# Feed-forward input transposes grouped by row tile instead of by column pair, in a decoder layer on one core

## The chip, the core and the metric

The kernel runs on one NeuronCore of a Trainium2 chip. The metric is the device time of one execution in microseconds (us). TensorE (PE in the profile; PEld is its weight load) multiplies matrices into PSUM, VectorE (DVE) and ScalarE (ACT) read PSUM and SBUF, GpSimd (POOL) works on SBUF, and SyncE (SP) issues nearly all DMA transfers. Each engine works through its own instructions in order and waits on semaphores for the others.

## What is computed

A decoder layer: each of three blocks is added to its input after a layer norm. The first is causal self-attention with ternary weights, the second attention over a context, the third a feed-forward block that sends each row to the best of eight low-rank experts.

```
x = x + self_attention(layernorm(x))                    # x: 16 x 256 x 1024, f32
x = x + cross_attention(layernorm(x), ctx, ctx)         # 16 heads of 64, causal
z = layernorm(x)
logits = z @ Wr.T + br                                  # Wr: 8 x 1024
weight, expert = max, argmax of softmax(logits)
h = einsum('nd,erd->ner', z, A)                         # A: 8 x 64 x 1024
y = einsum('ner,eor->neo', h, B) / 64                   # B: 8 x 1024 x 64
x = x + y[n, expert[n]] * weight
```

## The kernel before

The kernel has two halves, one after the other. The first (`self_attention`) does the self-attention and fills the time up to about 1650 us. The second (`second_half`, from line 1128) does the cross-attention and the feed-forward block, and the change is in it alone.

**Numbers.** A float32 value is held as two float16 halves, high and low, and a product is three float16 matmuls (`split_product`, L71 is its matmul). A transposed tile is made in PSUM; then ScalarE writes the high half to SBUF (`high`, L1493) and VectorE subtracts it from the bank for the low half (`low`, L1639), which frees the bank.

**Tiling.** One batch element has 256 rows, so two row tiles of 128, and 1024 columns, so eight column blocks of 128. It takes a *round* of eight steps, s0 to s7. Step g = 8b + s works on head pair s of batch element b: `scores` (L87, L91) on TensorE, the masked maxima on VectorE (L101), the exponentials on ScalarE (L108), the high halves of the probabilities on ScalarE (L1532) and the low ones on GpSimd (L1582), their transpose by DMA (L1315), and three steps later the weighted sums on TensorE (L118). Each of these engines runs one loop over g, written out by hand.

**Feed-forward in the same loop.** The tables `EXTRA` (TensorE), `HIGH_AHEAD` (ScalarE) and `LAST` (VectorE) say what of the feed-forward block of an earlier batch element goes into which step. In s5 TensorE does scores, weighted sums, the expert product e2 and then the transposes of the normalised input x3 into four PSUM banks, `("x", b, k)` for k = 0 to 3. In s6 it does scores, weighted sums and e3; in s7 scores, `logits` and weighted sums, then the first half of the hidden product h0, whose rest is in s0. `t0`, `t1` are the transposes of the hidden rows, `e0` to `e3` the products with B. All of these results go through five PSUM banks in a fixed turn (`claim`, `bank`, `freed`).

**The normalised tiles.** For batch element f, VectorE takes the statistics in s3, GpSimd the reciprocal root (L1560, L1563) in s4, and ScalarE writes x3, row tile 0 at the end of s4 and row tile 1 at the start of s5 (`norm_apply`, L1514), with a copy of the next values (L1508) between the two. Each raises `ln_done` by one. Before each of its four groups of transposes TensorE waits for both tiles:

```
if kind == "x":
    pe.wait_ge(ln_done, 2 * b + 2)
    transposes(x3, ("x", b, k))
```

A bank k holds column blocks 2k and 2k + 1 of both row tiles. So x3T, the transposed input, is filled by pairs of column blocks: `x3T[:, 0, 2k:2k+2, :]`, 512 numbers in a row for each partition. ScalarE copies the four banks in s6 ahead of the exponentials of s6, VectorE subtracts them in s6 after the maxima and the normalised sums. `logits` (s7) waits until the last of the four banks is freed, then multiplies row tile 0 and row tile 1 of x3T with the router's weights (L71, into ps_o): 24 products each.

**Keys and probabilities.** The context of batch element b + 1 is split into halves by ScalarE and GpSimd in s3 and s4, and SP transposes it by DMA into kT, one row tile in s5 and one in s6 (`transpose_keys`, L1348), ahead of the probabilities' transpose of the same step. In s6 a load of the following context (L1360) stands between. SP issues the probabilities' transpose of step g after GpSimd's low halves and after the weighted sums of g - 2. `scores` in s0 waits for the keys.

Of the kernel before, what the change touches and what calls it, by code (L numbers as in the profile page):

```python
# [14 lines left out]
ACT = mybir.ActivationFunctionType  # L15
AX = mybir.AxisListType

P = 128
NB = 16
T = 256  # L20
NT = T // P
# [43 lines left out]
def split_product(pe, out, lhs, rhs, n_tiles, part=None, exact=None):  # L65


    for a in part or range(n_tiles):
        terms = [t for t in ((0, 1), (1, 0), (0, 0)) if a > 0 or exact is None or t[exact] == 0]
        for t in terms:  # L70
            last = pe.matmul(out, lhs(t[0], a), rhs(t[1], a), start=a == 0 and t is terms[0],  # L71
                             stop=a == n_tiles - 1 and t == (0, 0))
    return last
# [1054 lines left out]
def second_half(nc, consts, banks, scratch, queries, ctx, begun, left, yT_last, out):  # L1128
    ident, mask = consts
# [7 lines left out]
    def sb(name, shape, dt=F32):  # L1137
        return st.enter_context(nc.sbuf_tensor(name, shape, dt))

    def sem(name):  # L1140
        return st.enter_context(nc.semaphore(name))
# [63 lines left out]
    with st:  # L1205
# [36 lines left out]
        x3T = sb("x3T", [P, 2, DT, T], F16)  # L1242
# [18 lines left out]
        j_ready = sem("j_ready2")  # L1261
        j_free = [sem(f"j_free2_{k}") for k in range(NBANK)]
        hi_done = sem("hi_done2")
# [14 lines left out]
        ln_done = sem("ln_done2")  # L1278
# [8 lines left out]
        def bank(c):  # L1287
            return ps_j[place[c] % NBANK]

        def ready(c):  # L1290

            return len([o for o in order[:place[c] + 1] if o[0] != "o"])

        def freed(c):

            return j_free[place[c] % NBANK], place[c] // NBANK + 1
# [86 lines left out]
        @block.tensor  # L1383
        def _(pe):
            def claim(c):
                if place[c] >= NBANK:
                    pe.wait_ge(*freed(order[place[c] - NBANK]))
                return bank(c)

            def transposes(src, c):  # L1390
                to = claim(c)
                for a in range(2):
                    for n in range(NT):
                        last = pe.transpose(to[:, bass.ts(a * NT + n, P)],
                                            src[:, n, bass.ts(2 * c[2] + a, P)], ident[:])
                last.then_inc(j_ready, 1)

            def scores(g):
                b, t = g // NPAIR, g % NPAIR
                slot = b % 2  # L1400
                if t == 0 and b > 0:
                    pe.wait_ge(*keys_in(b))
                    if b < NB - 1:
                        pe.wait_ge(qT_in[slot], 16 * ((b + 1) // 2))
                    else:
                        pe.wait_ge(q_last_in, 16 * NT)
                if g > 0:
                    pe.wait_ge(max_done, 4 * g)
                causal_scores(pe, ps_s,
                              lambda i, r, n: qT[slot][r, n, bass.ts(DT * i + t, P)],  # L1410
                              lambda i, r: kT[r, slot, i, t], s_ready)

            def weighted_sums(g):
                b, t = g // NPAIR, g % NPAIR
                if t == 0 and b > 0:
                    pe.wait_ge(v_done, 2 * b)
                if g > 0:
                    pe.wait_ge(y_done, g)
                pe.wait_ge(*transposed(g))
                for e in range(2):  # L1420
                    last = weights_times_values(pe, ps_o[:, e],
                                                lambda i, k: probT[:, g % 2, e, i, k],
                                                v[:, b % 2].rearrange(
                                                    "p n i (h d) -> p i n h d", d=HD),
                                                2 * t + e, HD)
                last.then_inc(o_ready, 1)

            def logits(f):
                pe.wait_ge(*freed(("x", f, 3)))
                pe.wait_ge(y_done, min(NPAIR * (f + 2) - 1 - SUMS, GP))  # L1430
                for n in range(NT):
                    last = split_product(pe, ps_l[:, n],
                                         lambda i, a: x3T[:, i, a, bass.ts(n, P)],
                                         lambda i, a: rT[:, i, a, :], DT)
                last.then_inc(l_ready, 1)

            def hidden(f, n, part):
                to = claim(("h", f, n)) if part is FIRST else bank(("h", f, n))
                last = split_product(pe, to[:], lambda i, a: x3T[:, i, a, bass.ts(n, P)],
                                     lambda i, a: aT[:, i, a, :], DT, part)  # L1440
                if part is SECOND:
                    last.then_inc(j_ready, 1)

            def hidden_transposes(f, n):
                to = claim(("t", f, n))
                pe.wait_ge(*freed(("h", f, n)))
                for a in range(ERT):
                    last = pe.transpose(to[:, bass.ts(a, P)], hg[:, n, bass.ts(a, P)], ident[:])
                last.then_inc(j_ready, 1)

            def expert_out(f, j):
                n, half = j // 2, j % 2
                to = claim(("e", f, j))
                pe.wait_ge(*freed(("t", f, n)))
                split_product(pe, to[:], lambda i, a: hT[:, i, n, a, :],
                              lambda i, a: bT[:, i, a, bass.ts(half, BANK)], ERT) \
                    .then_inc(j_ready, 1)

            def out_projection(j, a):
                to = claim(("o", NB - 1, j)) if a == 0 else bank(("o", NB - 1, j))  # L1460
                if (j, a) == (0, 0):
                    pe.wait_ge(yT_last, 16 * NT)
                last = split_product(pe, to[:], lambda i, a: yT[:, i, a, bass.ts(j // 2, P)],
                                     lambda i, a: woT[:, half_tile(i, a), bass.ts(j % 2, BANK)],
                                     DT, (a,), exact=1)
                if a == DT - 1:
                    last.then_inc(out_ready, 1)

            for g in range(GEND):
                if g < GP:  # L1470
                    scores(g)
                if g % NPAIR == NPAIR - 1 and 0 <= g // NPAIR - 1 < NB:
                    logits(g // NPAIR - 1)
                if 0 <= g - SUMS < GP:
                    weighted_sums(g - SUMS)
                for j, a in out_parts.get(g, []):
                    out_projection(j, a)
                for kind, b, k, part in listed(EXTRA, g):
                    if kind == "x":
                        pe.wait_ge(ln_done, 2 * b + 2)  # L1480
                        transposes(x3, ("x", b, k))
                    elif kind == "h":
                        hidden(b, k, part)
                    elif kind == "t":
                        hidden_transposes(b, k)
                    else:
                        expert_out(b, k)

        @block.scalar
        def _(act):  # L1490
            def high(dst, c):
                act.wait_ge(j_ready, ready(c))
                act.activation(dst, bank(c)[:], ACT.Copy).then_inc(hi_done, 1)  # L1493

            def pair(k):
                return slice(2 * k, 2 * k + 2)

            def high_of(c):
                kind, b, k = c
                if kind == "t":  # L1500
                    return hT[:, 0, k]
                return x3T[:, 0, pair(k), :]

            def values(b, n):
                act.wait_ge(ctx_in, 16 * b)
# [4 lines left out]
            def norm_apply(f, a):  # L1510
                act.wait_ge(ln_pow, 2 * f + 2)
                if f > 0:
                    act.wait_ge(j_ready, ready(("x", f - 1, 3)))
                act.activation(x3[:, a, :], x2[f % 3][:, a, :], ACT.Identity,  # L1514
                               scale=rstd[:, a:a + 1], bias=offset[:, a:a + 1]) \
                    .then_inc(ln_done, 1)
# [100 lines left out]
        def _(dve):  # L1617
# [18 lines left out]
            def low(dst, hi, c):  # L1636
                dve.wait_ge(hi_done, halves_done(c))
                src = bank(c)[:].rearrange("p (a n) -> p a n", a=hi.shape[1])
                dve.tensor_tensor(dst, src, hi, ALU.subtract).then_inc(freed(c)[0], 1)  # L1639

            def low_pair(to, c):
                a = slice(2 * c[2], 2 * c[2] + 2)
                low(to[:, 1, a, :], to[:, 0, a, :], c)

            def add_expert_out(f, j):
                c = ("e", f, j)
# [167 lines left out]
```

## Time and profile before

| | |
|---|---|
| median of 3 runs | 2278.14 us (2277.64 to 2280.89) |
| profiled execution | 2285.66 us |
| its span, first to last instruction | 2283.4 us |
| mean granted TensorE clock in it | 0.968 |
| TensorE busy | 2063.9 us (90%) |
| VectorE busy | 1642.1 us (72%) |
| ScalarE busy | 1172.9 us (51%) |
| GpSimd busy | 975.8 us (43%) |
| DMA, mean over the span | 163 GB/s |

All durations are of the one profiled execution. Busy shares are means over two halves with different loads: the second half begins at about 1650 us. The granted clock is the share of TensorE's full speed that the chip allowed in a stretch: 1.00 is 2.4 GHz, 0.50 is 1.2 GHz. Matmuls are pipelined, so a run of n of them is read from the start of one group to the start of the next. In a chain of waits each piece was released by the piece above it.

### The profile page before, as it was taken

How to read it: one execution, taken by the hardware profiler on the slowest of the kernel's cores; microseconds unless marked ns; L12 is line 12 of the kernel's file. 1: busy time of each engine (PE TensorE's matmuls, PEld its weight loads, DVE VectorE, ACT ScalarE, POOL GpSimd, SP SyncE). 2: the span in 40 equal slices, each digit the busy share in tenths (PEclk: the TensorE clock that was granted, in tenths of full speed). 3: DMA queues.
4: the chain of work that ended last, by engine and by line, in shares of the span. 5: the costliest groups of instructions: out<-in, count | busy, mean ns of one | idle time of the engine just before them, and what ended most of it. 6: DMA issues, size and time to landing. Idle time of an engine off the chain costs nothing. (4 is left out here: it accounts for less than half of the span.)

```text
span 2283.4 us, 52017 instructions
## 1 busy us (share of the span) xinstructions
PE 2063.9 (90%) x19320; PEld 1329.2 (58%) x19320; DVE 1642.1 (72%) x4595; ACT 1172.9 (51%) x3114; POOL 975.8 (43%) x919
## 2 busy tenths in 40 slices
PE   1657899999999999999999999997789899988978
PEld 1435566666666666666666666665345555554544
DVE  7877678777777777787777777766566667676664
ACT  6976434333433333333334334334677767686761
POOL 4333334334433333343343333433565656565651
PEclk9878999999999999999999999998899999999999
DMA  9977665665657666556556566568999999999862
GB/s 240 196 157 150 133 145 132 145 143 134 151 123 160 140 139 137 144 131 157 140 135 152 124 160 134 123 160 213 223 203 221 204 230 211 223 215 216 186 131 73
DMA packets 800572, 372.82 MB, mean 163 GB/s; under 512 B 746553, under 2 KB 746809, under 8 KB 800321
## 3 DMA queue, kind: packets, MB, share of 16 engines
q1 hardware_dynamic: 800320, 369.50, 71.1%
q8 instruction: 154, 2.52, 0.5%
q14 instruction: 98, 0.79, 0.1%
HBM read 104.11 MB, written 49.28 MB: 67 GB/s over the span
## 5 line engine op out<-in xcount | busy, mean ns | idle before, releaser
L108 ACT ACTIVATE prob<-prob,negmax 128x128 f32<-128x128 f32 (+1 forms) x1024 | 428.5, 444 | 175.0 <-DVE negmax L101 173.7
L905 POOL TENSOR_TENSOR halves<-prob,halves 128x384 f16<-128x384 f32 x256 | 239.7, 937 | 583.8 <-ACT halves L829 583.8
L71 PE MATMUL ps_j<-xT,wT 128*128 128x256 f16 x3634 | 416.6, 275 | 24.6 <-DMA wT<-rows_qkv 24.6
L101 DVE CUSTOM_DVE_ANT_0 prob<-ps_s,mask 128x128 f32<-128x128 f32 (+1 forms) x1024 | 304.3, 353 | 170.2 <-PE ps_s L91 170.0
L71 PEld LDWEIGHTS ps_j<-xT,wT 128*128 128x128 f16 x3634 | 359.0, 99 | 85.3 <-issue 24.8
L1062 DVE TENSOR_TENSOR raw<-raw,cos 128x512 f32<-128x512 f32 x128 | 140.4, 1097 | 249.7 <-DMA swp<-raw 249.7
L818 ACT ACTIVATE raw<-ps_j,factor_qk 128x256 f32<-128x256 f32 x158 | 66.2, 470 | 451.0 <-PE ps_j L71 451.0
L1582 POOL TENSOR_TENSOR halves<-prob,halves 128x768 f16<-128x768 f32 x128 | 210.7, 1646 | 174.1 <-ACT halves L1532 174.1
L71 PE MATMUL ps_t<-xT,wT 128*128 128x256 f16 x2254 | 255.5, 273 | 0.0
L71 PEld LDWEIGHTS ps_t<-xT,wT 128*128 128x128 f16 x2254 | 221.3, 98 | 36.4
L71 PE MATMUL ps_j<-wT,yT 128*128 128x512 f16 x897 | 205.4, 385 | 0.0
L71 PE MATMUL ps_j<-wT,xT 128*128 128x512 f16 x874 | 196.4, 381 | 0.0
L818 ACT ACTIVATE raw<-ps_t,factor_qk 128x256 f32<-128x256 f32 x98 | 41.1, 471 | 288.4 <-PE ps_t L71 288.4
L1064 DVE TENSOR_TENSOR swp<-swp,sin 128x512 f32<-128x512 f32 x128 | 172.4, 1347 | 0.0
L876 POOL TENSOR_TENSOR small<-small 128x1 f32<-128x1 f32 x62 | 34.4, 554 | 312.8 <-DVE small L1007 312.8
L71 PE MATMUL ps_t<-wT,xT 128*128 128x512 f16 x598 | 139.6, 391 | 7.6 <-DMA wT<-rows_qkv 7.6
L71 PEld LDWEIGHTS ps_j<-wT,yT 128*128 128x128 f16 x897 | 85.4, 99 | 98.2 <-issue 4.9
L899 POOL TENSOR_TENSOR yh<-y,yh 128x256 f16<-128x256 f32 x128 | 130.7, 1021 | 22.6 <-ACT yh L808 22.6
L71 PEld LDWEIGHTS ps_j<-wT,xT 128*128 128x128 f16 x874 | 83.4, 98 | 95.4 <-issue 2.1
L829 ACT ACTIVATE halves<-prob 128x384 f16<-128x384 f32 x256 | 133.8, 523 | 8.1
L71 PE MATMUL ps_t<-wT,yT 128*128 128x512 f16 x575 | 129.5, 381 | 0.0
L1532 ACT ACTIVATE halves<-prob 128x768 f16<-128x768 f32 x128 | 108.0, 843 | 37.4 <-DMA probT<-halves 34.0
(194 smaller groups left out, 3594.1 us busy)
## 6 DMA issues: line engine op xcount, KB each, us to landing
swp<-raw SPq DMA_DIRECT2D x512, 64.0 KB, 2.0
xin<-in_x SPq DMA_DIRECT2D x33, 512.0 KB, 4.4
kv_ahead<-in_ctx SPq DMA_DIRECT2D x16, 1024.0 KB, 6.3
x_kept<-after_self_attention SPq DMA_DIRECT2D x16, 1024.0 KB, 5.8
xres<-in_x SPq DMA_DIRECT2D x31, 512.0 KB, 4.3
after_self_attention<-xres SPq DMA_DIRECT2D x30, 512.0 KB, 3.3
queries<-q2T SPq DMA_DIRECT2D x30, 512.0 KB, 3.1
out<-x SPq DMA_DIRECT2D x10, 1024.0 KB, 5.0
```

The lines of the kernel that those rows point to most:

```text
L71: last = pe.matmul(out, lhs(t[0], a), rhs(t[1], a), start=a == 0 and t is terms[0], stop=a == n_tiles - 1 and t == (0, 0))
L101: dve.tensor_tensor_reduce(scores[:, cols], bank[:, cols], hidden, scale, NO_SCORE, ALU.add, ALU.min, least[:, n:n + 1]).then_inc(done, 1)
L108: last = act.activation(prob[:, cols], prob[:, cols], ACT.Exp, scale=-1.0, bias=least[:, n:n + 1], accum_out=None if sums is None else sum ...
L818: last = act.activation(raw[:, g % 2, w], bank(("qk", g, 0))[:, bass.ts(w, T)], ACT.Copy, scale=factor_qk[:, w, t:t + 1])
L829: act.activation(halves[:, e, 0, :], prob[:, e], ACT.Copy) \
L876: pool.tensor_tensor(rstd[:], rstd[:], minus_half[:], ALU.pow).then_inc(ln_pow, 1)
L899: pool.tensor_tensor(yh[:, :, 1, pair], y[:, g % 2], yh[:, :, 0, pair], ALU.subtract).then_inc(y_lo, 1)
L905: pool.tensor_tensor(halves[:, e, 1, :], prob[:, e], halves[:, e, 0, :], ALU.subtract).then_inc(prob_lo, 1)
L1062: dve.tensor_tensor(z, z, cos[:].unsqueeze(1).broadcast_to([P, 2, T]), ALU.mult) \
L1064: dve.tensor_tensor(swp[:], swp[:], sin[:].unsqueeze(1).broadcast_to([P, 2, T]), ALU.mult).then_inc(sin_done, 1)
L1532: act.activation(halves[:, g % 2, :, 0, :], prob[:, g % 2], ACT.Copy) \
L1582: pool.tensor_tensor(halves[:, g % 2, :, 1, :], prob[:, g % 2], halves[:, g % 2, :, 0, :], ALU.subtract).then_inc(prob_lo, 1)
```

## The change

A bank of the transposes now holds four column blocks of one row tile: banks 0 and 1 row tile 0 (blocks 0 to 3 and 4 to 7), banks 2 and 3 row tile 1. TensorE waits for tile 0 alone before banks 0 and 1, and for both before banks 2 and 3. ScalarE and VectorE write each bank to four pieces of 128 numbers in x3T, 256 apart. `logits` waits for banks 0 and 1 before row tile 0 and for banks 2 and 3 before row tile 1. ScalarE's `norm_apply` waits only for the transposes that read its own tile. The number of transposes, banks, copies and subtractions and their order are unchanged.

```diff
             def transposes(src, c):
+
+                n, first = c[2] // 2, 4 * (c[2] % 2)
                 to = claim(c)
-                for a in range(2):
-                    for n in range(NT):
-                        last = pe.transpose(to[:, bass.ts(a * NT + n, P)],
-                                            src[:, n, bass.ts(2 * c[2] + a, P)], ident[:])
+                for a in range(4):
+                    last = pe.transpose(to[:, bass.ts(a, P)],
+                                        src[:, n, bass.ts(first + a, P)], ident[:])
                 last.then_inc(j_ready, 1)
...
             def logits(f):
-                pe.wait_ge(*freed(("x", f, 3)))
                 pe.wait_ge(y_done, min(NPAIR * (f + 2) - 1 - SUMS, GP))
                 for n in range(NT):
+                    for k in (2 * n, 2 * n + 1):
+                        pe.wait_ge(*freed(("x", f, k)))
                     last = split_product(pe, ps_l[:, n],
...
                     if kind == "x":
-                        pe.wait_ge(ln_done, 2 * b + 2)
+                        pe.wait_ge(ln_done, 2 * b + 1 + k // 2)
                         transposes(x3, ("x", b, k))
...
             def high(dst, c):
                 act.wait_ge(j_ready, ready(c))
-                act.activation(dst, bank(c)[:], ACT.Copy).then_inc(hi_done, 1)
-
-            def pair(k):
-                return slice(2 * k, 2 * k + 2)
+                act.activation(dst, bank(c)[:].rearrange("p (a n) -> p a n", a=dst.shape[1]),
+                               ACT.Copy).then_inc(hi_done, 1)
...
-                return x3T[:, 0, pair(k), :]
+                return x3T[:, 0, bass.ts(k % 2, 4), bass.ts(k // 2, P)]
...
                 if f > 0:
-                    act.wait_ge(j_ready, ready(("x", f - 1, 3)))
+                    act.wait_ge(j_ready, ready(("x", f - 1, 2 * a + 1)))
...
             def low_pair(to, c):
-                a = slice(2 * c[2], 2 * c[2] + 2)
-                low(to[:, 1, a, :], to[:, 0, a, :], c)
+                a, n = bass.ts(c[2] % 2, 4), bass.ts(c[2] // 2, P)
+                low(to[:, 1, a, n], to[:, 0, a, n], c)
```

## Rows read from the trace of the kernel before

**Rows 1.** Windows: stretch, its us, busy us per engine, granted clock, DMA share, GB/s

```profile
1699.00:2171.00 472.00, 425.85 (x4897) 242.51 (x4898) 322.18 (x1320) 341.86 (x998) 287.19 (x241) 0.99 0.96 213
```

**Rows 2.** Waits of TensorE in 1700:2171: us in total, times, longest

```profile
PE ps_o L118 <- DMA probT<-halves: 11.5, 9, 2.4
PE ps_j L1394 <- ACT x L1514: 9.0, 7, 1.4
PE ps_t L1394 <- ACT x L1514: 6.5, 5, 1.4
PE ps_s L87 <- DMA kT_ahead<-v_ahead: 6.2, 7, 1.1
PE ps_o L71 <- DVE x3T L1639: 4.9, 12, 0.4
```

**Rows 3.** Timeline of TensorE: start, us, line, tiles, count, [idle before <- releaser]

```profile
1738.21 0.66 PE L1394 MATMUL ps_j<-ident,x 128*128 128x128 f32 x4 [0.88 <-ACT x L1514]
...
1776.86 0.66 PE L1394 MATMUL ps_t<-ident,x 128*128 128x128 f32 x4 [1.44 <-ACT x L1514]
...
1778.76 0.34 PE L87 MATMUL ps_s<-kT_ahead,qT_ahead 64*128 64x128 f16 x6
...
1783.65 1.36 PE L71 MATMUL ps_o<-rT_ahead,x3T 128*128 128x8 f16 x48 [0.41 <-DVE x3T L1639]
...
1818.30 1.09 PE L1394 MATMUL ps_j<-ident,x 128*128 128x128 f32 x8 [1.44 <-ACT x L1514]
```

**Rows 4.** Timeline of the other engines beside them, columns as in rows 3

```profile
1773.50 1.23 ACT L1514 ACTIVATE x<-x_kept,offset,rstd 128x1024 f32<-128x1024 f32 x1
...
1775.58 1.23 ACT L1514 ACTIVATE x<-x_kept,offset,rstd 128x1024 f32<-128x1024 f32 x1
...
1779.34 0.58 ACT L1493 ACTIVATE x3T<-ps_t 128x512 f16<-128x512 f32 x1
...
1781.72 1.88 DVE L1639 TENSOR_TENSOR x3T<-ps_j,x3T 128x512 f16<-128x512 f32 x3
```

**Rows 5.** Chain of waits in order of time, from 1738 us: start, us, what

```profile
1738.16 1.77 ACT prob L108 x8
...
1740.87 1.66 POOL halves L1582
1742.55 1.44 SPq L1315
1744.08 6.48 DMA kT_ahead<-v_ahead
...
1751.90 2.59 PE ps_j L71 x12
...
1764.08 2.76 PE ps_j L71 x12
```

**Rows 6.** Groups of the page: count, busy, mean ns of one, idle before

```profile
L1532 ACT ACTIVATE halves<-prob 128x768 f16<-128x768 f32 x128 | 108.0, 843 | 37.4 <-DMA probT<-halves 34.0
```

**Rows 7.** Timeline of TensorE at s0 and s1 of five rounds, columns as in rows 3

```profile
1750.61 0.34 PE L87 MATMUL ps_s<-kT_ahead,qT_ahead 64*128 64x128 f16 x6 [1.10 <-DMA kT_ahead<-v_ahead]
...
1794.96 1.12 PE L118 MATMUL ps_o<-v_ahead,probT 128*128 128x64 f16 x18 [2.39 <-DMA probT<-halves]
...
1950.85 0.69 PE L118 MATMUL ps_o<-v_ahead,probT 128*128 128x64 f16 x18 [1.71 <-DMA probT<-halves]
...
2023.08 0.34 PE L87 MATMUL ps_s<-kT_ahead,qT_kept 64*128 64x128 f16 x6 [0.71 <-DMA kT_ahead<-v_ahead]
...
2067.62 0.98 PE L118 MATMUL ps_o<-v_ahead,probT 128*128 128x64 f16 x18 [1.91 <-DMA probT<-halves]
```

**Rows 8.** Windows of 1 us behind three of these waits, columns as in rows 1

```profile
1795.00:1796.00 1.00, 1.00 (x19) 1.00 (x20) 0.00 (x0) 1.00 (x3) 0.17 (x1) 0.50 1.20 356
1951.00:1952.00 1.00, 1.00 (x21) 0.66 (x18) 0.40 (x2) 1.00 (x4) 0.29 (x1) 1.00 1.20 387
2068.00:2069.00 1.00, 1.00 (x14) 0.69 (x12) 0.33 (x2) 1.00 (x4) 0.51 (x1) 0.50 1.20 439
```

**Rows 9.** Chain of waits, from 1795 us

```profile
1796.08 3.68 PE ps_j L71 x12
```

## The prediction, written before the changed kernel ran

> **What bounds the kernel now.** I read the windows first, then TensorE's waits, then one round of the second half in order of time, and last the chain of waits. A round is the eight steps s0 to s7 of one batch element. In the twelve full rounds between 1699 and 2171 us TensorE is busy for 425.85 of 472 us and the DMA engines 0.96 of it [rows 1]: both are nearly full, so only the order of the waits can say which sets the pace.
>
> TensorE's waits in these twelve rounds [rows 2]: 15.5 us for ScalarE's normalised tile before the transposes of the feed-forward input (9.0 + 6.5, once a round), 4.9 us for the low half of x3T before the logits (once a round), 6.2 us for the transposed keys at s0 (seven times) and 11.5 us for transposed probabilities (nine times). The change goes at the first two.
>
> In order of time [rows 3, 4]: ScalarE ends tile 0 at 1774.73 (start 1773.50 + 1.23) and tile 1 at 1775.58 + 1.23 = 1776.81, with a values copy between them. TensorE comes to the transposes at 1776.86 - 1.44 = 1775.42, when tile 0 is 0.7 us old, and waits for tile 1. The sixteen transposes then run until the next scores at 1778.76, which is 1.90 us. At the logits it waits 0.41 us more.
>
> The chain of waits tells which of this matters [rows 5]. After tile 1 (end about 1738.16) it goes through ScalarE's exponentials of s5, GpSimd's low halves, SP's issue of the probabilities' transpose, SP's issue of the second key transpose at 1744.08 and its landing 6.48 us later, at 1750.56. TensorE starts s0 at 1750.61. From there to the expert product of s3 (1764.08) it is TensorE's own matmuls, then VectorE's statistics, ScalarE, and tile 1 again at 1776.81: 38.65 us, which is also the distance between the transposes of two rounds (1738.21 and 1776.86) [rows 3]. **TensorE's transposes, e3 and the logits (s5 to s7) are not on this loop**; they lie beside ScalarE, GpSimd, SP and the key transpose.
>
> **The change, part by part.**
>
> *Transposes.* Sixteen before, sixteen after, same shape, same four banks in the same order: 0. The first two banks now need tile 0 alone. They take half of 1.90, so 0.95 us, and start at 1775.42, in what was a stall. TensorE then waits 1776.86 - 1775.42 - 0.95 = 0.49 us, and the other two banks end 0.95 us earlier than before. Nine of the twelve waits are like this one (1.43 or 1.44); in the other three (0.78 to 0.94; 1738.21 shows 0.88 [rows 3]) the wait goes whole.
>
> *ScalarE's copies and VectorE's subtractions.* Four of each a round, still 128x512 from one bank. ScalarE is not helped: when it comes to them at 1779.34 the banks have been full since 1778.76, so its chain from tile 1 through the exponentials and these copies stays where it is [rows 4, 5]. VectorE begins its subtractions after the maxima of s6, which need TensorE's scores of s6; these come 0.95 us earlier. At the start-to-start spacing of the rows (0.6 us) the last then ends near 1782.7 in place of 1783.6 (1781.72 + 1.88) [rows 4].
>
> *The output pattern.* The copies wrote 512 numbers in a row; now they write four pieces of 128 with gaps. No row shows this form from PSUM. The nearest is the copy of the probabilities' high halves, which writes 768 numbers in two pieces with a gap: 843 ns, or 1.10 ns a number [rows 6], against 0.58 us for 512, or 1.13, in a row [rows 4]. From that the new form costs 0.02 us less a copy at best. At worst I let the same 0.02 us be the cost of each of three gaps: 0.06 us a copy, some 0.25 us a round. I take 0, and even the 0.25 lies behind the point in s5 where the loop leaves ScalarE for GpSimd.
>
> *The logits' waits.* One wait becomes four, two of them between the two tiles. Tile 0 has 24 of the 48 products, half of 1.36 us [rows 3]. TensorE arrives at 1783.24 - 0.95 = 1782.3; banks 0 and 1 are subtracted by about 1781.4, the last by 1782.7, before tile 0's products end at 1783.0. So the wait of 0.41 goes. Three more waits cost between 0 and the 0.41 they replace, off the loop; I take 0.
>
> *The other waits.* ScalarE's wait for the banks of the round before is satisfied some 35 us earlier: 0. On SP nothing is moved. Its transposes of s5 and s6 and the key transposes wait for GpSimd and for its own queue, not for work that TensorE does between the transposes and s0. That is why no DMA starts earlier.
>
> So TensorE reaches s0 earlier by 0.95 + 0.41 = 1.36 us in each round, and if this were on the path it would be 9 x 0.95 + 2.60 + 4.9 = 16.1 us in all. But s0 waits for the keys, which land as before. **The stall moves**: 1.10 becomes 1.10 + 1.36 = 2.46 us in one piece. Six of the seven key waits are between 0.71 and 1.13 (1750.61 and 2023.08 stand in [rows 7]) and become 2.07 to 2.49. In the other rounds the wait at s1 for the probabilities, issued behind the key transpose, takes it back. None of the twelve rounds is without one of the two.
>
> **What is late next is the clock.** After the waits of 2.39 us at 1794.96 and of 1.91 at 2067.62 the granted clock stands at 0.50, which is 1.2 GHz; it is 1.00, 2.4 GHz, after the wait of 1.71 at 1950.85 [rows 7, 8]. Before all three TensorE had been busy for microseconds. The twelve matmuls behind the first of them took 3.68 us [rows 9] against 2.59 in an ordinary round [rows 5]. That round lasted 1818.30 - 1776.86 = 41.44 us [rows 3]; less 38.65 and less the longer stall (2.39 - 1.10 = 1.29) that leaves 1.50 us for one fall of the clock. It falls on s0 and s1, which are on the loop.
>
> The sum against the profiled execution: 2285.66 (span 2283.4 and 2.26 around it) + 6 x 1.50 = 2294.7. That execution is 7.5 us above the median of the runs; the difference has nothing to do with the change, so the forecast is 2278.14 + 9.0 = **2287.1 us**.
>
> The Trainium skill (TensorE: Matmul & The Clock Gate, "Why this matters for your kernels") speaks against this term: it has the clock fall only after idle gaps that are longer than any expected here, and by it the sum would be 2278.1. The trace disagrees, with 0.50 behind gaps of 2.39 and 1.91 [rows 7, 8].
>
> **The rivals.**
>
> *Nothing measurable (2278.1).* The moved stalls of 2.1 to 2.5 us leave the clock up, or the keys land 0.4 us or more earlier once rounds are longer, which keeps the stalls under 2 us. For it: 1.71 did no harm, and the new stalls may be cut in two by s0's short work where the keys come early. Against it: 1.91 and 2.39 did harm, and the new stalls, 2.07 to 2.49, are all above 1.91. That the change does not do what it says is unlikely: tile 0 is ready before TensorE comes [rows 3, 4].
>
> *Faster (between 2262.0 and 2278).* TensorE with 425.85 of 472 us could be the real bound, with the DMA landing at s0 and s1 following it. Then all 16.1 us are kept: 2278.1 - 16.1 = 2262.0; half kept is 2270. For it: the landing varies from round to round (no key wait in five rounds), so part of it is crowding that an altered order may ease, and the probabilities of s7 can be issued earlier where s0 is. Against it: the chain does not pass through s5 to s7 in ordinary rounds [rows 5], and the issue of the keys hangs on ScalarE.
>
> *Slower still (2291.6).* Nine of the twelve rounds show no fall now (three have one, behind waits of 2.39, 1.91 and one more of that size). If all nine fall: 9 x 1.50 = 13.5. It takes over from the forecast where waits for probabilities also grow past 2 us in one piece.
>
> **How the numbers follow.** A difference of 0.2% (4.6 us) is what a measurement of this kernel can tell from none. Forecast, falls in some four to eight rounds (2284 to 2290): 0.38. Slower still: 0.12. Nothing: 0.29. Faster: 0.21, most of it between 2266 and 2273. So slower 0.50, same 0.29, faster 0.21. The range 2270 to 2294 leaves out about 0.1 below (most of the gain kept) and under 0.1 above (falls in all rounds and a dearer copy).
>
> **What the profile after would show.** The transposes' wait split, with about 0.5 us before the third bank; no wait for x3T before the logits; tile 1 to the key landing still some 12.4 us; key waits above 2 us and clock 0.50 behind them. The step fails if the key waits do not grow (then the landing followed TensorE: faster), or if they grow and the clock stays at 1.00 (then same). A transposes' wait still of 1.44 would mean that the order of banks does not do what I read.

## The result

| | before | changed |
|---|---|---|
| median of 7 runs | 2278.14 us (2275.84 to 2288.05) | 2285.87 us (2282.29 to 2289.10) |
| profiled execution, its span | 2285.66 us, 2283.4 us | 2283.42 us, 2281.3 us |

The ratio is 1.0028, with a 95% interval of 1.0015 to 1.0041: slower by 6.4 us (the two medians lie 7.7 us apart), against a forecast of 9.0. A second comparison gave 1.0025 (1.0014 to 1.0035). The two profiled executions stand the other way round, because the first half of the kernel, which is the same in both, happened to be some 5 us shorter in the profile of the changed kernel (its first transposes come at 1653.4 in place of 1658.3). The comparison below is therefore made over the twelve full rounds of the second half.

The waits of TensorE in these rounds of the changed kernel (us in total, times, longest), to be held against [rows 2]:

```profile
PE ps_o L118 <- DMA probT<-halves: 20.3, 14, 3.0
PE ps_s L87 <- DMA kT_ahead<-v_ahead: 16.2, 12, 2.5
...
PE ps_j L1395 <- ACT x L1514: 3.6, 7, 0.6
PE ps_t L1395 <- ACT x L1514: 2.3, 4, 0.6
```

The wait for the normalised tiles is 5.9 us where it was 15.5, and the one for x3T before the logits (4.9) is gone. The wait for the keys is 16.2 where it was 6.2, and the one for the probabilities 20.3 where it was 11.5. So 14.5 us of waiting left s5 to s7, and 18.8 us arrived at s0 and s1.

One round of the changed kernel, the transposes of s5 and what follows (timeline of TensorE), to be held against [rows 3]:

```profile
1769.56 0.60 PE L1395 MATMUL ps_t<-ident,x 128*128 128x128 f32 x4
1769.99 0.60 PE L1395 MATMUL ps_j<-ident,x 128*128 128x128 f32 x4
1771.16 1.09 PE L1395 MATMUL ps_j<-ident,x 128*128 128x128 f32 x8 [0.57 <-ACT x L1514]
...
1776.61 1.36 PE L71 MATMUL ps_o<-rT_ahead,x3T 128*128 128x8 f16 x48
```

The first two banks run while ScalarE writes tile 1, the wait before the third is 0.57 us, and the logits start without one.

And s0 and s1 of three rounds, to be held against [rows 7] (timeline of TensorE):

```profile
1744.12 0.34 PE L87 MATMUL ps_s<-kT_ahead,qT_ahead 64*128 64x128 f16 x6 [1.45 <-DMA kT_ahead<-v_ahead]
...
1749.34 0.69 PE L118 MATMUL ps_o<-v_ahead,probT 128*128 128x64 f16 x18 [0.73 <-DMA probT<-halves]
...
1789.14 0.69 PE L118 MATMUL ps_o<-v_ahead,probT 128*128 128x64 f16 x18 [2.99 <-DMA probT<-halves]
...
1825.12 0.34 PE L87 MATMUL ps_s<-kT_ahead,qT_ahead 64*128 64x128 f16 x6 [2.54 <-DMA kT_ahead<-v_ahead]
```

Six of the twelve rounds are like the first: the stall comes in two pieces, 1.4 to 1.7 us for the keys and 0.7 to 1.2 for the probabilities, and the clock stays up. Windows of one us behind the last two waits (busy us per engine, then granted clock, DMA share, GB/s):

```profile
1826.00:1827.00 1.00, 1.00 (x19) 0.65 (x16) 1.00 (x9) 0.49 (x3) 0.00 (x0) 1.00 1.45 211
1790.00:1791.00 1.00, 1.00 (x4) 0.31 (x3) 0.46 (x2) 1.00 (x5) 0.99 (x1) 0.50 1.06 438
```

It fell behind 2.99, at s1, and did not behind 2.54, at s0. All four falls in these rounds stand behind waits for the probabilities at s1 (2.99, 2.45, 2.87 and 2.66 us), none behind a wait for the keys.

### What a round is made of

Taking the end of tile 1 on ScalarE as the start of a round, every round of every traced kernel splits into two parts. The second, from the start of the weighted sums of s1 to the end of the next tile 1, is 21.77 us in most rounds: 23.1 to 23.5 where the clock fell behind the wait at s1, 0.1 to 0.7 more in one or two rounds of each kernel (four in the changed kernel with both moves, below), and once, in the kernel of before with both moves, 2.0 more without a fall. All else that the change and the experiments do is in the first part, which ends when TensorE has reached those weighted sums *and* the probabilities of s6 have landed. Where only the keys are late, it is the start of s0 plus 4.42 us.

The next table is worked out from the timelines of TensorE, ScalarE and SP, for twelve rounds of each kernel. The first part is the twelve rounds less 12 x 21.77 and less 1.6 us for each fall, divided by 12. "Issued late" counts the rounds in which SP issued the transpose of the probabilities of s6 over 9.8 us after tile 1; otherwise it does so at 9.2 to 9.6. Read from the traces round by round instead, the mean of the first part is 17.06 and 17.00 us in the two profiles of before and 17.34 in both of the changed kernel.

| kernel | TensorE at s0, earlier by | twelve rounds | falls | first part, mean | issued late | ratio |
|---|---|---|---|---|---|---|
| before, first profile | 0 | 471.3 us | 3 | 17.10 us | 2 | |
| before, second profile | 0 | 467.3 | 1 | 17.04 | 1 | 0.9996 |
| layout only | -0.1 us | 469.2 | 2 | 17.06 | 0 | 0.9999 |
| both tiles awaited | 0.5 | 472.7 | 3 | 17.22 | 3 | 1.0020 |
| logits whole | 0.7 | 469.5 | 2 | 17.09 | 4 | 1.0014 |
| changed, first profile | 1.3 to 1.4 | 476.0 | 4 | 17.37 | 8 | 1.0028 |
| changed, second profile | 1.3 to 1.4 | 474.1 | 3 | 17.34 | 8 | 1.0025 |

### The profile page after: what moved, and what is told of

Its sections match the earlier page's. It is cut to its first block and busy times, and to the rows that moved or that the text cites. A ratio compares the mean times of both kernels' runs of the same rounds, so it can differ in the third digit from the quotient of the medians.

```text
span 2281.3 us, 52033 instructions
## 1 busy us (share of the span) xinstructions
PE 2062.1 (90%) x19320; PEld 1329.5 (58%) x19320; DVE 1646.3 (72%) x4595; ACT 1170.7 (51%) x3114; POOL 974.9 (43%) x919
```

## The experiments

Each was timed in interleaved rounds against the kernel before; "before" in a ratio is always that kernel.

### The changed kernel again, and the kernel before again

> The changed kernel again, beside the others on one chip. Measured so far: ratio to before 1.0028 (1.0015 to 1.0041). Expected 1.003 again, some 6 us above before. In the trace: in the twelve full rounds of the second half the waits before the transposes near 0.57 us each, those for keys and probabilities at s0 and s1 together above 2 us a round, and more falls of the granted clock than the three of before.

Measured: 2286.43 us against 2280.10, ratio 1.0025 (1.0014 to 1.0035). The waits were as expected; the falls in the twelve rounds were three, no more than in the first profile of before.

> The kernel before, unchanged, for a second profiled execution: the first one (2285.66 us) lay above the median of its runs. Expected ratio 1.000. In the trace either the same three falls of the clock in the twelve full rounds and about 471 us for these rounds (then the surplus of the first profile lies in the first half), or fewer and a shorter stretch (then the profile of before overstated its falls).

Measured: ratio 0.9996 (0.9986 to 1.0006). The second profile has one fall and 467.3 us for the twelve rounds, so the first one, which the prediction rested on, overstated the falls of before: one to three, not three. The first parts of the two agree within 0.06 us.

### The layout alone

The edit is against the changed kernel, as are the next three.

```diff
+                pe.wait_ge(*freed(("x", f, 3)))
                 for n in range(NT):
-                    for k in (2 * n, 2 * n + 1):
-                        pe.wait_ge(*freed(("x", f, k)))
...
-                        pe.wait_ge(ln_done, 2 * b + 1 + k // 2)
+                        pe.wait_ge(ln_done, 2 * b + 2)
...
-                    act.wait_ge(j_ready, ready(("x", f - 1, 2 * a + 1)))
+                    act.wait_ge(j_ready, ready(("x", f - 1, 3)))
```

> The new bank layout and output pattern alone: TensorE waits for both tiles before the transposes and for the last bank before the logits, and ScalarE's wait is that of before. TensorE reaches s0 when it did before. Theory (only the earlier arrival at s0 and s1 costs): ratio 1.000, 2280 us, with the old waits of 1.44 and 0.41 us and the old key waits. Rival (the pattern in four pieces costs the most, since the variant that waits for both tiles still measured 1.0020): ratio 1.002. Between, about 1.001: each has a share.

Measured: 2281.69 us against 2280.00, ratio 0.9999 (0.9988 to 1.0010). The waits are back at 1.44 and 0.50 us. The four pieces cost nothing that shows: by the tile x3T in the traces, a subtraction takes 680 ns (median) in the changed kernel and 681 before, a copy 598 ns against 597 to 599, with the same spread of 577 to 616.

### Both tiles awaited, logits split

```diff
-                        pe.wait_ge(ln_done, 2 * b + 1 + k // 2)
+                        pe.wait_ge(ln_done, 2 * b + 2)
```

> The changed kernel with one thing undone: before all four groups of transposes TensorE waits for both tiles (ln_done 2b + 2), as before. The new bank layout, the output pattern and the split logits waits stay. Theory (the moved stall and the clock falls behind it cost the time): the stall of 1.44 us is back at the transposes, the waits at s0 and s1 shrink by 0.95 us, and the time is that of before, 2278 to 2280 (ratio 1.000 to 1.001). Rival (the output pattern in four pieces or the added waits cost it): ratio 1.003 as in the changed kernel, with longer copies of x3T in the trace.

Measured: 2286.41 us against 2280.10, ratio 1.0020 (1.0010 to 1.0031). The expectation of 1.000 to 1.001 was wrong. TensorE is earlier at s0 by no more than the logits' wait, and still most of the loss is there. The rival named with it falls too, with the layout alone at 0.9999. What the expectation overlooked is that the loss is not in proportion to the time gained: in the trace TensorE waits 9.6 us for keys and 15.0 for probabilities in place of 6.2 and 11.5, and three rounds are issued late.

### Tiles one by one, logits whole

```diff
+                pe.wait_ge(*freed(("x", f, 3)))
                 for n in range(NT):
-                    for k in (2 * n, 2 * n + 1):
-                        pe.wait_ge(*freed(("x", f, k)))
```

> The changed kernel with the logits waiting for the last bank before row tile 0, as before; the transposes wait for the tiles one by one. TensorE gains 0.95 us at the transposes and, since the banks are freed at about 1.36 us less than its old arrival, at most a few tenths of wait are left at the logits: arrival at s0 is 1.0 to 1.3 us earlier. Theory (earlier arrival costs, by way of longer waits and falls): ratio 1.0015 to 1.003. Rival (the split of the logits is the costly part, since it is what the variant with both tiles kept): ratio 1.000 to 1.001.

Measured: 2283.31 us against 2280.00, ratio 1.0014 (1.0003 to 1.0025). Between nothing (layout alone) and the whole change. A wait of 0.50 us is left at the logits in every round, so TensorE comes to s0 only 0.7 us earlier and not 1.0 to 1.3. The intervals of this one, of the one above and of the whole change overlap, so their order among each other is not shown. The interval of each kernel that brings TensorE forward lies above 1.000, that of the layout alone does not, though it overlaps with this one's. The trace here shows none of the loss: its twelve rounds, 469.5 us, lie between those of the two profiles of before, and its profiled execution is 1.7 us below the median of its runs.

### Work put into the stall

```diff
+            def filler(c, n_tiles):
+                kind, f, n = c
+                to = claim(c)
+                terms = [(i, j, a) for a in range(n_tiles) for i, j in ((0, 1), (1, 0))]
+                for m, (i, j, a) in enumerate(terms):
+                    pe.matmul(to[:], x3T[:, i, a, bass.ts(n, P)], aT[:, j, a, :],
+                              start=m == 0, stop=m == len(terms) - 1)
...
+                if g % NPAIR == 1 and 0 <= g // NPAIR - 2 < NB:
+                    filler(("h", g // NPAIR - 2, 1), 2)
                 if 0 <= g - SUMS < GP:
                     weighted_sums(g - SUMS)
```

> The changed kernel with four matmuls of 512 columns more a round, 0.87 us of work whose result nothing reads: TensorE does them in s1 between the scores and the weighted sums, inside the wait for the probabilities of s6. Theory (falls of the clock behind idle stretches cost part of the time): the waits at s1 shrink by 0.87 us, those of 2.4 to 3.0 go below 2.1, the three to five falls in the twelve rounds become none to two, and the kernel is 3 to 7 us faster than the changed one in spite of the added work. Rival (the falls cost nothing because the landing of the probabilities sets the pace anyway): within 2 us of the changed kernel. Rival (TensorE's work is the bound): 16 x 0.87 = 14 us slower.

Measured: 2284.94 us against 2280.10, ratio 1.0017 (1.0007 to 1.0027), 1.5 us below the changed kernel of the same comparison, a difference that the two intervals don't separate from none. The falls went from three or four to one, as expected, and the twelve rounds of the trace take 472.3 us in place of 476.0 and 474.1. The gain was to be 3 to 7 us and is smaller, within the first rival's 2 us. The added work did not cost its 14 us, so it lies in a stall. That falls of the clock are a part of the loss is thus read from the traces; the times neither show it nor speak against it.

### Both key transposes in s5

```diff
-                if s in (5, 6) and b + 1 < NB:
-                    transpose_keys(b + 1, s - 5)
+                if s == 5 and b + 1 < NB:
+                    transpose_keys(b + 1, 0)
+                    transpose_keys(b + 1, 1)
```

> The changed kernel with SP issuing both key transposes in s5 ahead of the probabilities of s5, instead of the second in s6. Theory (the landing of keys and probabilities behind the chain from tile 1 sets the pace, TensorE's s5 to s7 do not): the keys land about 3 us earlier from tile 1, the waits for them at s0 go (17 us in the changed kernel), and so the 1.36 us a round that the change takes from s5 to s7 begin to count: faster than before by 5 to 20 us, if the probabilities of s6 do not become the later ones at s1. If they do, the waits at s1 grow by what those at s0 lose and the time stays at the changed kernel's.

> The kernel before with both key transposes issued in s5, the twin of the changed kernel so edited, which measured 0.9963. Theory (the landing of the probabilities of s6 at s1 sets the pace in both, TensorE's s5 to s7 do not count): no key wait at s0, the transposes' wait of 1.44 and the logits' of 0.41 stay, the waits at s1 are some 1.3 us shorter than in the twin (0 to 1.9 in place of 0.9 to 3.2), fewer falls, and the ratio is 0.992 to 0.997, equal to the twin or better. Rival (with the keys early TensorE's path counts, and the change is a gain there): ratio 0.998 to 1.000, slower than the twin by 4 us or more.

Measured: 2274.16 us, ratio 0.9963 (0.9947 to 0.9979) with the change; 2271.74 us, ratio 0.9956 (0.9943 to 0.9968) without it. The two intervals overlap. The key waits went (0.2 us in all with the change), the waits for the probabilities took their place (25.2 us with the change, 11.9 without), and the change is still no gain. Of the two stalls at s0 and s1, removing one leaves the other. Of the two outcomes in the first expectation it is the second that came at s1, though the kernel did get faster with the keys out of the way. The second expectation held: no key waits, waits at s1 of 0.1 to 1.8 us, no fall in the twelve rounds, and its rival (0.998 to 1.000) is false.

### The load of the context behind the probabilities of s6

```diff
-                if s == 6 and b + 2 < NB:                # ahead of the other transfers of s6
-                    sp.wait_ge(v_done, 2 * (b + 1))
-                    sp.dma_start(kv[:], ctx_t[b + 2]).then_inc(ctx_in, 16)
...
                 transpose_probabilities(g)
+                if s == 6 and b + 2 < NB:
+                    sp.wait_ge(v_done, 2 * (b + 1))
+                    sp.dma_start(kv[:], ctx_t[b + 2]).then_inc(ctx_in, 16)
```

> The changed kernel with the load of the context alone moved behind the probabilities' transpose of s6; the second key transpose stays in s6. Theory: the keys land at 11 to 12.5 us from tile 1 as before or up to 1 us earlier for want of the load beside them, the probabilities of s6 are issued at about 9 us and land before TensorE's s0 + 4.42, rounds of 37.0 to 38.2 us, no falls, ratio 0.992 to 0.996; still no gain over its twin of before, because s0 waits for the keys in both. Rival (the bytes are the bound): ratio above 1.000.

> The kernel before with the load of the context alone moved behind the probabilities' transpose of s6. Theory: as its twin with the change, ratio 0.991 to 0.996, and within 3 us of it, since the key landing at s0 sets the pace in both.

Measured: 2256.73 us, ratio 0.9909 (0.9893 to 0.9924) with the change; 2264.68 us, ratio 0.9941 (0.9927 to 0.9955) without. The kernel of before came out as expected. The changed one is faster than its range of 0.992 to 0.996, and the claim that the two would be equal was wrong: with the load out of the way the change is a gain of 8 us, and the two intervals don't touch. One fall came where none was expected, behind a wait for the keys of 2.63 us at s0. In the trace TensorE starts s0 at 11.45 us after tile 1 on average, against 11.91 in the twin. Part of it is rounds in which the keys land at 10.8, which is before TensorE's arrival in the twin (11.27), so that TensorE decides there and the keys here; part is that in other rounds the keys land near 11.6 in the changed kernel where they land at 12.4 in the other.

### Both moves

The two edits above together, on SP alone.

> The changed kernel with both key transposes in s5 and the load of the context issued behind the probabilities' transpose of s6 instead of ahead of it. In every traced kernel so far a round is the distance from the end of tile 1 to the start of the weighted sums of s1, plus 21.77 us (23.3 behind a fall of the clock). Theory: that distance is the later of TensorE's own arrival (s0 + 4.42 us, with s0 at 9.93 in the changed kernel and 11.27 in that of before) and the landing of the probabilities of s6. With the 1 MB load out of the way of that landing (15.1 to 17.6 so far) TensorE's own arrival at 14.35 decides, and the change is a gain at last: rounds of 36.1 to 36.6 us, ratio 0.982 to 0.988, and 8 to 16 us faster than its twin of before. Rival (the bytes are the bound, the load only delays later transposes): ratio 0.993 to 0.997, no difference to the twin.

> The kernel before with the same two moves on SP. Theory: TensorE reaches the weighted sums of s1 at 11.27 + 4.42 = 15.69 us from tile 1 and waits for nothing there, rounds of 37.5 us, ratio 0.990 to 0.993, slower than the changed kernel's twin by 8 to 16 us. Rival (the bytes are the bound): equal to the twin at 0.993 to 0.997.

Measured: 2246.42 us, ratio 0.9859 (0.9844 to 0.9874) with the change; 2257.69 us, ratio 0.9912 (0.9898 to 0.9926) without. The change gains 11.3 us, inside the 8 to 16 expected. Both ratios are inside their ranges. Ten of the twelve rounds without the change are 37.5 us as expected; those with it are 36.1 to 37.5 in place of 36.1 to 36.6, because in six of them TensorE waits 0.4 to 0.8 us at s0 for the probabilities of s5.

One round of the kernel of before with both moves, and one of the changed kernel with both (chain of waits):

```profile
1767.43 1.04 ACT v_ahead L1509
1768.48 1.14 ACT x L1515
1769.66 0.66 PE ps_t L1395 x4
1770.32 1.31 PE ps_j L1395 x12
1774.01 1.51 DVE x3T L1640 x3
1775.72 0.69 DVE x3T L1640
1776.46 1.36 PE ps_o L71 x48
1777.82 0.54 PE ps_o L118 x18
1778.36 2.59 PE ps_t L71 x12
```

```profile
1765.37 1.14 ACT x L1515
1766.55 1.09 PE ps_j L1396 x8
...
1768.88 2.59 PE ps_t L71 x12
...
1772.07 1.29 PE ps_o L71 x48
1773.36 0.54 PE ps_o L118 x18
1773.90 2.59 PE ps_t L71 x12
```

In the first the chain runs where [rows 5] did not: from tile 1 through TensorE's transposes, VectorE's subtractions and the logits, with no DMA in it. These are exactly the two waits that the change shortens. From the transposes to the logits it takes 1776.46 - 1769.66 = 6.80 us. In the second only two of the four banks stand behind tile 1, TensorE's own e3 follows, and the logits come 1772.07 - 1766.55 = 5.52 us after.

The waits of TensorE between 1690 and 2130 us, in the first and in the second (about twelve rounds in the second, somewhat less in the first):

```profile
PE ps_j L1395 <- ACT x L1515: 10.8, 8, 1.4
PE ps_t L1395 <- ACT x L1515: 5.1, 4, 1.4
PE ps_o L71 <- DVE x3T L1640: 4.9, 12, 0.4
...
PE ps_o L118 <- DMA probT<-halves: 3.7, 4, 1.3
```

```profile
PE ps_o L118 <- DMA probT<-halves: 10.0, 14, 1.3
...
PE ps_s L87 <- DMA kT_ahead<-v_ahead: 0.7, 3, 0.3
```

The weighted sums of s1 start 15.70 us after tile 1 in every round without the change (11.27 + 4.42), and at 14.34 to 15.57 with it, where 9.93 + 4.42 = 14.35 is the least. Twelve rounds take 452.3 and 439.6 us, with no fall of the clock in either. The changed kernel with both moves is the fastest kernel of this study, 1.4% below the kernel before.

## Why the prediction was right, point by point

**The bound, and where the gain goes: right, and shown.** The prediction said that TensorE's s5 to s7 lie beside a chain that ends in the landing of keys and probabilities, and that what the change gains there is waited for again at s0 and s1. The waits of the changed kernel show it, and the pair with both moves shows the reverse: with that landing out of the way, the same change gains 11.3 us of the 16.1 that the prediction worked out for it "if this were on the path".

**The gain at the transposes and the logits: right.** A rest of 0.57 us was seen for 0.49, the logits' wait is gone, TensorE comes to s0 1.3 to 1.4 us earlier for 1.36, and the output pattern costs nothing that shows (layout alone: 0.9999, 0.9988 to 1.0010).

**The moved stall in one piece: wrong.** The prediction kept the key landing at 12.4 us from tile 1 and so expected 2.07 to 2.49 us in one wait at s0 in six rounds. None of these six looks so: the keys land 0.3 to 1.1 us earlier there than before, TensorE waits 1.4 to 1.9 us for them in the two profiles, and the rest of the stall stands at s1, before the probabilities of s6. One other round, which had no wait for keys before, has 2.54 and 2.46. The rival "nothing measurable" had named this: keys that land 0.4 us or more earlier and keep the stalls under 2 us.

**The clock: wrong place and wrong count, right price.** Six more falls at 1.50 us each, behind the waits for the keys at s0, were to give 9.0 us. The price was right (the second part of a round is 23.1 to 23.5 in place of 21.77, so 1.3 to 1.7). The place was not: no fall of the changed kernel stands behind a wait for the keys, not even behind the 2.54 us, which by the prediction's own sign should have had 0.50 behind it. (In the kernel with the load alone moved one fall does stand behind a wait for keys, of 2.63 us.) Nor was the count: four and three falls in the two profiles of the changed kernel, three and one in the two of before, all at s1, so 1.5 more on average, or 2.4 us in twelve rounds.

**What made up the sum instead.** The first part of a round grew from 17.04 and 17.10 us to 17.34 and 17.37, which is 0.28 x 12 = 3.4 us. With the falls that is 5.8 us for the twelve rounds, which is by construction their difference in the traces; the whole kernels differ by 5.7 to 6.4. So the forecast is near the result in part by luck: it had 9.0 us of falls where 2.4 came, and nothing for the 3.4 us of later landings. The term that the prediction lacked is on SP, whose issues it had called unmoved. Its order is; its times are not. One round of before and one of the changed kernel (timeline of SP's queue):

```profile
1742.55 1.44 SPq L1315 DMA_TRANSPOSE probT<-halves  x1
1744.08 2.50 SPq L1348 DMA_TRANSPOSE kT_ahead<-v_ahead  x1
1746.63 0.68 SPq L1360 DMA_DIRECT2D kv_ahead<-in_ctx  x1
1747.40 6.70 SPq L1315 DMA_TRANSPOSE probT<-halves  x2
```

```profile
1737.05 1.44 SPq L1315 DMA_TRANSPOSE probT<-halves  x1
1738.58 3.34 SPq L1348 DMA_TRANSPOSE kT_ahead<-v_ahead  x1
1741.97 0.57 SPq L1360 DMA_DIRECT2D kv_ahead<-in_ctx  x1
1742.64 5.80 SPq L1315 DMA_TRANSPOSE probT<-halves  x2
```

With tile 1 ending at 1738.16 and 1732.67, the second key transpose is issued 5.92 and 5.91 us after it in both. Its issue then takes 2.50 us in the one and 3.34 in the other, so the probabilities of s6, behind the context's load, follow at 9.24 and at 9.97. The keys land earlier and the probabilities later. The key transpose takes over 3 us to issue in eight and seven rounds of twelve in the two profiles of the changed kernel, in one of twelve in each of before, in none with the layout alone, and in three and four with one half of the change.

**What goes along with the long issue** stands in the traces too. The profile counts 154 packets of 16 KB on a queue of its own, `q8 instruction`, beside the data on q1. The microsecond that begins 6.0 us after the end of tile 1, in the same round of before and of the changed kernel (DMA view: packets, MB, their time as a share of the 16 engines'):

```profile
q1 hardware_dynamic: 835, 0.21, 114.8%
```

```profile
q1 hardware_dynamic: 694, 0.18, 256.0%
q8 instruction: 1, 0.02, 6.5%
```

And that microsecond with the next one, before and changed (windows, columns as in [rows 1]):

```profile
1744.16:1745.16 1.00, 0.59 (x17) 0.30 (x11) 1.00 (x3) 0.97 (x3) 0.00 (x0) 1.00 1.15 214
1745.16:1746.16 1.00, 1.00 (x46) 1.00 (x44) 1.00 (x6) 0.21 (x2) 0.73 (x1) 1.00 1.13 204
```

```profile
1738.67:1739.67 1.00, 1.00 (x45) 1.00 (x42) 1.00 (x6) 0.97 (x3) 0.00 (x0) 1.00 2.62 194
1739.67:1740.67 1.00, 1.00 (x18) 0.64 (x15) 0.97 (x9) 1.00 (x6) 0.74 (x1) 1.00 0.06 6
```

With the instruction packet, the data packets around it take more than twice their time, and next to nothing moves in the microsecond after it (6 GB/s where before had 204). The transposed probabilities of s5, under way at that time, land 4.7 us after their issue in place of 3.8 (DMA view, before and changed):

```profile
probT<-halves SPq DMA_TRANSPOSE x1, 3.8
```

```profile
probT<-halves SPq DMA_TRANSPOSE x1, 4.7
```

SP's issue of the key transpose behind them ends within 0.6 us of that landing, in every round. In the ten traces in which SP's order up to the keys is that of before, 120 rounds, the issue takes over 3 us exactly in the 40 rounds in which an instruction packet starts 5.5 to 8.2 us after tile 1; in the 80 others none does. The kernel before has one such round in each profile too.

Where the packet falls goes along with how far ahead TensorE is. Nine rounds of before have one between 5 and 11 us after tile 1. With the layout alone eight of these nine keep it within 0.8 us of its old place. In the changed kernel seven of them have it 1.5 to 2.8 us earlier, which takes it from the transfer of the keys (at 8.4 to 10.4 us) into that of the probabilities of s5. In the eight rounds of the changed kernel with a long issue (first profile; one of them has it before as well) the probabilities of s6 land 0.3 to 1.1 us later than in the same round before, in the four others within 0.15 us of before, and the eight hold 2.9 of the 3.4 us. The landing of the keys shows the packets too: in the 29 of the 120 rounds without one between 5 and 10.7 us after tile 1 the keys land at 10.5 to 10.8 us, and the 12.4 us that the prediction took as fixed are found only in rounds with one.

**What stays open.** No run moves the instruction packet alone, so that it causes the long issue, and the long issue the later landing, is read from traces and not shown by an edit. That it carries TensorE's own program is inferred from its place going along with TensorE. Why it holds up the data packets is not shown. The moves on SP shift the load and the keys together and so don't isolate it.

**The rivals.** "Nothing measurable" is outside the interval of the ratio. "Faster", with TensorE as the real bound, is false for this kernel, and true for the same kernel once SP issues the context's load later. The rule of the Trainium skill that was weighed (TensorE: Matmul & The Clock Gate, "Why this matters for your kernels"), by which only longer gaps let the clock fall, is not borne out here either way round: in the two kernels clocks of 0.50 stand behind waits of 1.91 to 3.32 us, and 1.00 behind others of 1.93, 2.54 and 2.82. The longest wait at s0 or s1 with 1.00 behind it in the twelve rounds of any trace, 3.08 us, is in the changed kernel with both key transposes in s5 (timeline of TensorE, then the window behind it):

```profile
1791.97 0.69 PE L118 MATMUL ps_o<-v_ahead,probT 128*128 128x64 f16 x18 [3.08 <-DMA probT<-halves]
```

```profile
1793.00:1794.00 1.00, 1.00 (x6) 0.41 (x5) 0.33 (x1) 1.00 (x7) 1.00 (x1) 1.00 1.10 455
```

## What to carry to other kernels

Before a stall on a busy engine is shortened, follow the chain of waits over one whole period: a wait that the chain does not pass, 1.44 us every 38.65 us here, is slack, and taking it away moves it to the next landing on the path. Find the constant part of the period (21.77 us here) and what ends the other part; that told in one number per round what each edit did. And when an edit brings no gain because something else is late, try it again after that is mended: the same lines cost 6 us here and gained 11 once a key transpose had moved ahead of the probabilities of s5 and the context's load behind those of s6. A kernel whose engines run ahead of their old time can also meet transfers that nobody wrote into the program: look at every DMA queue of the profile, not only at the one that the kernel's own issues use.

## What was not expected of the hardware

- A wait's length alone did not decide whether the granted clock fell: it went to 0.50 behind waits of 1.91 and 1.96 us in one profile, and stayed at 1.00 behind 2.54 and 3.08 in others. Each fall here made the round 1.3 to 1.7 us longer.
- The same DMA transpose of keys, issued by SP 5.9 us after tile 1 behind the same transfers, took SP 2.0 to 2.7 us to issue in 80 rounds and 3.2 to 4.1 in 40, with nothing between. The 40 are those with a 16 KB packet of the queue `q8 instruction` 5.5 to 8.2 us after tile 1.
- A load of 1 MB issued ahead of a transpose rather than behind it cost 15 us in a kernel of 2280 (0.9941 in the kernel of before): the probabilities of s6 landed 6.6 to 8.8 us behind their issue with the load in front, and 3.7 to 4.8 us with it behind them.
